# A Mamba-style decoder layer on one core: the FFN residual moved into TensorE and ScalarE, the FFN in float32, and the convolution in packed halves

## The chip, the core and the metric

The kernel runs on 1 core of one Trainium2 chip. The metric is the device time of one execution in microseconds. The kernel before takes 1060.97 us (median of 3 runs, 1060.91 to 1061.49). The engines are TensorE (PE), VectorE (DVE), ScalarE (ACT), GpSimd (POOL) and SyncE (SP), which here issues nearly all DMAs.

## The reference

Four sequences of 512 tokens and 512 features go through three blocks, each of the form `x = layernorm(x + f(x))`:

```
proj = einsum('blh,he->bel', x, W_in);  hidden, gate = split(proj)       # 1024 channels each
hidden = silu(causal_conv4(hidden) + conv_bias)                          # depthwise, 4 taps
dt, B, C = split(hidden @ W_x);  dts = softplus(dt @ W_dt + b_dt)
state[t] = exp(dts*A) * state[t-1] + dts*B*hidden;  y = sum_n state*C    # 1024 channels x 16 states
f1 = ((y + hidden*D) * silu(gate)) @ W_out                               # block 1
f2 = x @ softmax((ctx Wq + bq)(ctx Wk + bk)^T)^T                         # block 2
x_scale = max|x row|/127;  x_q = round(x/x_scale);  w_q = round(w/w_scale)   # block 3, the FFN
f3 = (x_q @ w_q^T) * x_scale * w_scale + bias
```

## The kernel before

The work of one sequence ("batch" below, 0 to 3) is cut into 32 units. A unit is 32 channels times 16 states, laid out as 128 partitions by 4 groups of 512 time steps. For each unit SP copies the step sizes and inputs of 32 channels four times over the partitions (`rep<-steps`, line 357), ACT makes `dA` with four exponentials (line 553), DVE multiplies (`dBu`, line 776, two halves) and runs the recurrence (line 784, two halves), POOL multiplies the states by C (line 447), and after four units PE adds up the states with a 0/1 matrix (`state_sum`, key `y`, lines 938 and 944). DVE finishes the four units with `hs = y * gate` (line 750).

The program is one static list of steps `(b, g)`, `g` from 0 to 31. At step g of batch b, DVE does unit 32b + g + 1 and ACT the exponentials of the unit after that. Beside them each step has "items", given by the tables `REST`, `HID_AT`, `CONV_AT` and the order in `items()`: the projections and the convolution of the batch after (`h`, `c`, `g`, `z`) and attention and FFN of the batch before (`wo`, `q`, `k`, `en`, `at`, `xt`, `av`, `qt`, `ff`). All engines walk the same list of items in order, and the four PSUM banks `dense0` to `dense3` are given to the items in turn. So an engine that is late with an item holds up everything behind it on its own queue, and a product four items later.

Parts that the change touches:

- Convolution (`c`): ACT copies the projected channels from PSUM to `pj` (line 529); PE then multiplies four 128x128 diagonal matrices of taps with `pj` shifted by 0 to 3 steps (line 975).
- FFN (`qt`, `ff`): ACT rounds the rows (`xq`, line 602), PE transposes them (`qt`), ACT turns them into bf16 integers (line 566), PE multiplies with the bf16 integer weights (`ff`), and DVE scales by row and column (line 880) and adds the residual with its row sum (line 714, `add_rows`). POOL has added the bias to the residual before (line 476). Then come the moments on ACT, `rstd` on POOL, and the normalization on ACT (line 587).
- `wp`: the first six of eight channel blocks of the last batch's output projection, added to x by DVE (line 864).
- Batch 3 has nothing beside its scan but attention and FFN of batch 2, then its own rest comes alone at the end (`REST_BESIDE`, `REST_AFTER`).

Of the kernel before, what the change touches and what calls it, by code (L numbers as in the profile page):

```python
# [5 lines left out]
ALU = mybir.AluOpType  # L6
# [5 lines left out]
P = 128  # L12
NB = 4
# [16 lines left out]
REPS = 4  # L30
RING = 6
# [11 lines left out]
REST = {"wo": [3, 3, 6, 8], "q": [2], "k": [1], "en": [5, 9, 10, 11], "at": [10, 12, 14, 14],  # L43
        "xt": [13, 13, 14, 15], "av": [15, 17, 19, 19], "qt": [18, 20, 22, 23], "ff": [19, 22, 23, 25]}
REST_BESIDE = {"q": [22], "k": [22], "en": [23, 23, 26, 27], "at": [26, 27, 28, 29], "wp": [27, 28, 29, 30]}
REST_AFTER = {"wo": [3, 4, 5, 6], "xt": [5, 6, 7, 8], "av": [6, 7, 8, 9], "qt": [9, 10, 11, 12],
              "ff": [10, 11, 12, 13]}

HID_AT = [5, 9, 11, 13, 14, 17, 19, 22]
CONV_AT = [9, 10, 13, 14, 17, 18, 21, 24]  # L50
# [18 lines left out]
def items(b, g):  # L69
# [13 lines left out]

    if after and g == (B_AT if b >= 0 else 27):
        keys.extend(("sb", b + 1, j) for j in range(NJ))
# [6 lines left out]
    if after and b >= 0:  # L92
        keys.extend(("c", b + 1, i) for i, at in enumerate(CONV_AT) if at == g)
# [4 lines left out]
    if b == LAST:  # L98
        rest(b, REST_BESIDE, ("q", "k", "at", "en", "wp"))
    if after and g == DT_AT:  # L100
        keys.append(("dt", b + 1, 0))
# [7 lines left out]
    if b == 0 and g == 4:  # L109
        keys.append(("ws", 0, 0))  # L110
    if g % 4 == SUM_AT and 0 <= n - 1 < NB * NE:
        keys.append(("y", (n - 1) // NE, (n - 1) % NE))
# [24 lines left out]
def decoder_layer(nc, x, xT, ctxT, w_in, w_conv, conv_k, conv_b, w_x, w_dt, b_dt, w_out, a_log, d_skip,  # L137
# [9 lines left out]
    with ExitStack() as ctx:  # L147
# [9 lines left out]
        WfT = sb("WfT", [P, KH, H], BF16)  # L157
        ident = sb("ident", [P, P])
        sel = sb("sel", [P, P])
# [13 lines left out]
        ws_bc = sb("ws_bc", [P, H])  # L173
# [3 lines left out]
        steps = sb("steps", [P, 3, 2, T])  # L177
# [5 lines left out]
        pj = sb("pj", [P, T])  # L183
        dA = sb("dA", [P, 2, NJ, T])
# [26 lines left out]
        xqT = small[:, 2 * T:3 * T].bitcast(BF16).rearrange("p (s k t) -> p s k t", s=2, k=KH)  # L211
        wide_scale = small[:, 0:KH * P].rearrange("p (k c) -> p k c", k=KH)
# [12 lines left out]
        xsc = sb("xsc", [P, TT])  # L225
        xinv = sb("xinv", [P, TT])
# [6 lines left out]
        s_act_c = sem("act_constants_loaded")  # L233
        s_wx = sem("wx_loaded")
# [43 lines left out]
        s_xb = sem("ffn_bias_added")  # L278
        s_ln3 = sem("ln3_done")
# [38 lines left out]
        def _(sp):  # L318
# [50 lines left out]
            for b, g in STEPS:  # L369
# [4 lines left out]
                for key in items(*STEPS[STEPS.index((b, g)) - 1]) if (b, g) != STEPS[0] else ():  # L374
                    if key[0] in "hgc":
                        load_w(wuse.index(key) + 3)
# [734 lines left out]
```

## Time and profile before

| | us |
|---|---|
| median of 3 runs | 1060.97 |
| the profiled execution | 1060.82 |
| its span in the trace | 1059.0 |
| DVE busy | 984.8 (93%) |
| PE busy | 864.7 (82%) |
| ACT busy | 806.3 (76%) |
| POOL busy | 734.5 (69%) |
| mean granted TensorE clock | 0.913 of full |

The first scan starts at 54 us and the last ends at 1009 us. The batches start their scans about 245 us apart, batch 0 after 221 us already since no batch stands before it. A row of the timeline reads: start, duration, engine, line, operation, out<-in, count, and in brackets the idle time of the engine before it with what ended that. A full-precision (float32) matmul of 512 columns shows as two records.

### The profile page before, as it was taken

What the parts mean: (1) busy time and instruction counts of PE and PEld (TensorE: products, weight loads), DVE (VectorE), ACT (ScalarE), POOL (GpSimd) and SP (SyncE); (2) the same over time, 40 slices, a digit from 0 to 9 for tenths busy, and PEclk for the clock granted to TensorE, in tenths of its full rate; (3) what the DMA queues carried; (4) which work ended last, traced back from release to release, by engine and by line L of the source; (5) the groups of instructions that cost most, each with busy time, mean ns of one, the idle gap of its engine ahead of it and who ended that gap; (6) DMA issues with size and microseconds to landing.
All of it is one profiled execution on the core that took longest, in us unless ns stands there. A gap on an engine that the chain in (4) does not pass through costs nothing.

```text
span 1059.0 us, 10554 instructions
## 1 busy us (share of the span) xinstructions
PE 864.7 (82%) x3078; PEld 352.8 (33%) x3088; DVE 984.8 (93%) x813; ACT 806.3 (76%) x1222; POOL 734.5 (69%) x260
## 2 busy tenths in 40 slices
PE   8955788876899899977699899967799576767895
PEld 3321233321344343322244344432234242323432
DVE  3699999999999999899999999899999999999747
ACT  4486788876778898998767898997876886986424
POOL 1057777777787766688778866588778867878443
PEclk9988799888899999978899999989799879878998
DMA  6255444554743344343744544344743443244001
GB/s 197 78 125 133 102 120 129 122 132 115 196 126 88 101 129 119 80 116 102 231 125 100 129 120 109 79 106 130 213 115 90 133 106 90 70 129 110 1 0 40
DMA packets 58473, 120.08 MB, mean 113 GB/s; under 512 B 12208, under 2 KB 18480, under 8 KB 58416
## 3 DMA queue, kind: packets, MB, share of 16 engines
q1 hardware_dynamic: 57696, 119.34, 43.0%
q8 instruction: 25, 0.41, 0.1%
q14 instruction: 32, 0.26, 0.1%
q10 hardware_dynamic: 720, 0.08, 0.1%
HBM read 48.07 MB, written 4.19 MB: 49 GB/s over the span
## 4 chain that ended last, share of the span: by engine, by line
DVE 32%; issue 31%; PE 18%; ACT 13%; DMA 2%; SPq 2%; POOL 2%; DVEq 0%; POOLq 0%; ACTq 0%
DVE st L784 21%; PE dense L897 10%; DVE dBu L776 7%; ACT dA L553 4%; PE dense L944 3%; ACT L553 2%; DMA rep<-steps 2%; PE dense L975 2%; SPq L357 1%; POOL st L447 1%; ACT L543 1%; DVE dense L880 1%; DVE xsc L840 1%; PE dense L926 1%; PE dense L919 1%
## 5 line engine op out<-in xcount | busy, mean ns | idle before, releaser
L447 POOL TENSOR_TENSOR st<-st,Cb 128x2048 f32<-128x2048 f32 x127 | 649.4, 5113 | 266.8 <-DVE dBu L776 265.9
L784 DVE TENSOR_TENSOR_SCAN st<-dA,dBu 128x1024 f32<-128x1024 f32 x256 | 570.1, 2266 | 0.4 <-ACT dA L553 0.4
L553 ACT ACTIVATE dA<-rep,Aneg 128x511 f32<-128x511 f32 x512 | 328.2, 710 | 53.7 <-DVE st L784 49.4
L776 DVE TENSOR_TENSOR dBu<-rep,Bb 128x1024 f32<-128x1024 f32 x256 | 305.2, 1236 | 1.9 <-DMA rep<-steps 1.9
L897 PE MATMUL dense<-xTs,Win 128*128 128x512 f32 x504 | 237.0, 617 | 7.9 <-ACT wide L558 5.1
L944 PE MATMUL dense<-st,sel 128*32 128x512 f32 x1024 | 139.2, 691 | 57.7 <-POOL st L447 57.0
L897 PEld LDWEIGHTS dense<-xTs,Win 128*128 128x128 f32 x504 | 99.8, 200 | 137.5 <-issue 136.8
L897 PE MATMUL dense<-wide,hs 128*128 128x512 f32 x256 | 114.7, 601 | 1.9 <-DVE hs L750 1.0
L553 ACT ACT_TABLE_LOAD x78 | 100.1, 1283 | 9.7 <-DVE st L784 8.5
L975 PE MATMUL dense<-pj,Win 128*128 128x512 f32 (+1 forms) x192 | 87.6, 599 | 1.7 <-ACT pj L529 0.9
L944 PEld LDWEIGHTS dense<-st,sel 128*32 128x32 f32 x1024 | 33.4, 124 | 158.3 <-issue 89.8
L465 POOL TENSOR_TENSOR rstd<-var,neghalf 128x1 f32<-128x1 f32 x48 | 36.5, 759 | 49.1 <-DVE var L733 27.5
L897 PEld LDWEIGHTS dense<-wide,hs 128*128 128x128 f32 x256 | 49.1, 194 | 63.5 <-issue 63.5
L897 PE MATMUL dense<-dt_s,Wdt 128*128 128x512 f32 x64 | 38.4, 685 | 28.0 <-ACT Bb L558 19.4
L975 PEld LDWEIGHTS dense<-pj,Win 128*128 128x128 f32 x192 | 35.2, 190 | 53.0 <-issue 53.0
L587 ACT ACTIVATE x<-x,nmean,rstd 128x512 f32<-128x512 f32 x36 | 28.6, 809 | 26.0 <-POOL nmean L467 26.0
L897 PE MATMUL dense<-wide 128*128 128x512 f32 x96 | 45.2, 621 | 0.5 <-ACT steps L543 0.5
L543 ACT ACT_TABLE_LOAD x32 | 41.1, 1283 | 0.6
L648 ACT ACT_TABLE_LOAD x32 | 41.1, 1283 | 0.6
L750 DVE TENSOR_TENSOR hs<-dense,ta 128x512 f32<-128x512 f32 x32 | 21.4, 668 | 20.9 <-PE dense L944 20.9
L938 PE MATMUL dense<-hs,Ddiag 128*128 128x512 f32 x64 | 33.3, 602 | 6.2 <-ACT Cb L558 4.4
L897 PE MATMUL dense<-hs,wide 128*128 128x512 f32 x80 | 35.8, 597 | 1.8 <-ACT hs L534 1.4
(120 smaller groups left out, 778.7 us busy)
## 6 DMA issues: line engine op xcount, KB each, us to landing
rep<-steps SPq DMA_DIRECT2D x512, 128.0 KB, 2.4
Win<-w_in SPq DMA_DIRECT2D x64, 256.0 KB, 2.9
wide<-w_out SPq DMA_DIRECT2D x4, 2048.0 KB, 9.7
Win<-w_conv SPq DMA_DIRECT2D x24, 256.0 KB, 2.9
xTs<-xT SPq DMA_DIRECT2D x3, 1024.0 KB, 5.7
x<-x SPq DMA_DIRECT2D x3, 1024.0 KB, 8.5
out<-x SPq DMA_DIRECT2D x12, 256.0 KB, 2.0
wide<-w_x SPq DMA_DIRECT2D x4, 640.0 KB, 5.0
```

The source lines that it names most:

```text
L447: nc.gpsimd.tensor_tensor(s, s, Cb[:], ALU.mult).then_inc(s_p, NH)
L465: nc.gpsimd.tensor_tensor(rstd[:, c], var[:, c], neghalf[:], ALU.pow).then_inc(s_rstd, 1)
L543: nc.scalar.activation(steps[:, n % 3, 0, :], ps, ACT.Softplus, bias=bdt[:, e:e + 1]).then_inc(free, 1)
L553: nc.scalar.activation(dA[:, u % 2, j, 1:T], rep[:, u % REPS, 0, 1:T], ACT.Exp, scale=Aneg[:, u % UNITS, j:j + 1]).then_inc(s_dA, 1)
L587: nc.scalar.activation(x_i, x_i, ACT.Identity, scale=rstd[:, n % 4:n % 4 + 1], bias=nmean[:, n % 4:n % 4 + 1]).then_inc({"wo": s_ln1, "av" ...
L648: nc.scalar.activation(temp_slot(key), ps, ACT.Silu).then_inc(free, 1)
L776: V.tensor_tensor(dBu[:, j, :], rep[:, u % REPS, 1:2, :].to_broadcast([P, JH, T]), Bb[:, j, :], ALU.mult).then_inc(s_mul, 1)
L784: V.tensor_tensor_scan(st[:, u % RING, j, :].rearrange("p j t -> p (j t)"), dA[:, u % 2, j, :].rearrange("p j t -> p (j t)"), dBu[:, j, :] ...
L897: mm = nc.tensor.matmul(ps[0:rows, :], lhsT, rhs, start=n == 0, stop=n == len(pairs) - 1)
L938: nc.tensor.matmul(ps, Ddiag[:, e, :], hs[:, b % 2, e, :], start=True, stop=False)
L944: mm = nc.tensor.matmul(ps[32 * q:32 * q + 32, :], sel[:, 0:32], st[:, (4 * n + q) % RING, j, :], start=False, stop=j == NJ - 1)
L975: mm = nc.tensor.matmul(ps[:, k:T], Win[:, n % 3, k, :], pj[:, 0:T - k], start=k == 0, stop=k == KC - 1)
```

## The change

- FFN in float32: the weights stay rounded, but are multiplied by their scale again (so they carry the column scale) and kept in float32, as are the rounded rows. The matrix `ws_bc` of column scales and its products go away.
- FFN residual, batches 0 to 2: at `qt`, ACT waits for POOL's bias add and multiplies the residual row in place by `1/x_scale` (new semaphore `s_xs`). PE adds it into the product with an identity matmul. ACT evicts the sum, scaled by `x_scale`, with its row sum. DVE has no part in it any more. Batch 3 keeps DVE's add, with the row scale in the same instruction.
- `wp`: PE adds x by an identity matmul, ACT copies the result.
- Convolution in halves: SP copies `pj` by four DMAs into `pk`, in which each half of 64 channels stands twice, the second copy shifted by one step. Two matrices of 64 output columns per half then cover four taps, so there are two pairs of 64-column matmuls instead of four of 128. Tap DMAs are half as large.
- `steps` has 2 buffers instead of 3 (`DTS`). `xqT` is twice as large and overlaps `bc_s`, so the copy `bc` waits for the last `ff` of the batch before the last.
- Tables and order: `y` now stands first in its step (it was last), `c` behind the rest, and most tables have moved by a step or so.
- The last unit's second half is multiplied by C on DVE, not on POOL.

```diff
-HID_AT = [5, 9, 11, 13, 14, 17, 19, 22]
-CONV_AT = [9, 10, 13, 14, 17, 18, 21, 24]
+HID_AT = [6, 9, 12, 13, 14, 16, 18, 21]
+CONV_AT = [9, 10, 13, 14, 16, 19, 21, 24]
...
+            def shift_taps(b, i):
+                n = NE * (b - 1) + i
+                product_read(sp, ("h", b, i))
+                if n:
+                    product_done(sp, ("c", (n - 1) // NE + 1, (n - 1) % NE))
+                else:
+                    sp.wait_ge(s_prep, 1)
+                for m in range(2):
+                    half = slice(64 * m, 64 * m + 64)
+                    sp.dma_start(pk[0:64, m, :], pj[half, :]).then_inc(s_pk, 16)
+                    sp.dma_start(pk[64:128, m, 1:T], pj[half, 0:T - 1]).then_inc(s_pk, 16)
...
                 if n:
-                    product_done(act, ("c", (n - 1) // NE + 1, (n - 1) % NE))
+                    act.wait_ge(s_pk, 64 * n)
                 nc.scalar.copy(pj[:], ps).then_inc(free, 1)
...
                     elif kind == "qt":
                         integers(key, xqT[:, i % 2])
+                        if kb < LAST:
+                            act.wait_ge(s_xb, TT * kb + i + 1)
+                            x_i = rows_of[kb][:, i, :]
+                            nc.scalar.activation(x_i, x_i, ACT.Identity, scale=xinv[:, i:i + 1]).then_inc(s_xs, 1)
+                    elif kind == "wp":
+                        copied(key, rows_of[kb][:, i, :], lambda ps: ps)
+                    elif kind == "ff" and kb < LAST:
+                        ps, free = full(key)
+                        n = norm[key]
+                        nc.scalar.activation(rows_of[kb][:, i, :], ps, ACT.Identity, scale=xsc[:, i:i + 1],
+                                             accum_out=rowsum[:, n % 4:n % 4 + 1]).then_inc(free, 1)
...
-                        link(V.scalar_tensor_tensor(ps, ps, xsc[:, i:i + 1], ws_bc[:], ALU.mult, ALU.mult))
                         dve.wait_ge(s_xb, TT * kb + i + 1)
-                        add_rows(key, x_i, ps, free)
+                        add_rows(key, x_i, ps, free, xsc[:, i:i + 1])
...
-                        for k in range(KC):
-                            mm = nc.tensor.matmul(ps[:, k:T], Win[:, n % 3, k, :], pj[:, 0:T - k],
-                                                  start=k == 0, stop=k == KC - 1)
+                        for k in range(0, KC, 2):
+                            for m in range(2):
+                                mm = nc.tensor.matmul(ps[64 * m:64 * m + 64, k:T],
+                                                      Win[:, n % 3, k // 2, 64 * m:64 * m + 64],
+                                                      pk[:, m, 0:T - k], start=k == 0, stop=k == KC - 2)
...
                         product_read(pe, ("qt", kb, i))
-                        product(key, [(xqT[:, i % 2, k, :], WfT[:, k, :]) for k in range(KH)])
+                        rows = []
+                        if kb < LAST:
+                            pe.wait_ge(s_xs, TT * kb + i + 1)
+                            rows = [(ident[:], rows_of[kb][:, i, :])]
+                        product(key, [(xqT[:, i % 2, k, :], WfT[:, k, :]) for k in range(KH)] + rows)
```

TensorE, steps 18 to 20 of batch 1 or 2, before (`small x4` is `qt`, `wide` is `av`, `WfT` is `ff`, `Ddiag` and `st,sel` are `y`, `pj` is `c`, `xTs,Win` is `h` or `g`):

```order
L919 MATMUL dense<-ident,small 128x128 x4
L897 MATMUL dense<-xTs,Win 128x512 x4
L897 MATMUL dense<-wide 128x512 x8
L897 MATMUL dense<-WfT,small 128x512 x4
L897 MATMUL dense<-xTs,Win 128x512 x4
L919 MATMUL dense<-ident,small 128x128 x4
L938 MATMUL dense<-hs,Ddiag 128x512
L944 MATMUL dense<-st,sel 32x512 x16
```

The same place in the kernel after, and on to the first `ff`, which is now at step 21:

```order
L947 MATMUL dense<-ident,small 128x128 x4
L925 MATMUL dense<-wide 128x512 x8
L1004 MATMUL dense<-pk,Win 64x512 x2
L1004 MATMUL dense<-pk,Win 64x510 x2
L925 MATMUL dense<-xTs,Win 128x512 x4
L966 MATMUL dense<-hs,Ddiag 128x512
L972 MATMUL dense<-st,sel 32x512 x16
L947 MATMUL dense<-ident,small 128x128 x4
L925 MATMUL dense<-xTs,Win 128x512 x4
L925 MATMUL dense<-WfT,small 128x512 x4
L925 MATMUL dense<-x,ident 128x512
```

Here `y` stands ahead of its step's `qt`, and `ff` has moved behind it, with the identity matmul of the residual at its end.

ScalarE, step 22 of batch 1 or 2, before (with the semaphores that each row waits for):

```order
L543 ACTIVATE steps<-dense,bdt 128x512 [waits dense_full1]
L529 COPY pj<-dense 128x512 [waits dense_full0,dense_full2]
L566 ACTIVATE small<-dense,unround 128x512 [waits dense_full3]
L553 ACT_TABLE_LOAD [waits scan_done]
L553 ACTIVATE dA<-rep,Aneg 128x511 [waits rep_loaded1]
```

The same step in the kernel after:

```order
L558 ACTIVATE steps<-dense,bdt 128x512 [waits dense_full1]
L581 ACTIVATE small<-dense,unround 128x512 [waits dense_full2]
L699 ACTIVATE x<-x,winv 128x512 [waits ffn_bias_added]
L706 ACTIVATE x,rowsum<-dense,wscale 128x512 [waits dense_full3]
L602 ACTIVATE x<-x,nmean,rstd 128x512 [waits rstd_ready]
L568 ACT_TABLE_LOAD [waits scan_done]
L568 ACTIVATE dA<-rep,Aneg 128x511 [waits rep_loaded1]
```

Two full-row instructions stand between the transposed rows and the next exponentials, and the first of them waits for POOL.

TensorE, steps 28 and 29 of batch 3, before (`ident,xTs` is `at`, `wide,hs` is `wp`):

```order
L926 MATMUL dense<-ident,xTs 128x128 x3
L929 MATMUL dense<-ident 128x128
L926 MATMUL dense<-ident,xTs 128x128
L897 MATMUL dense<-wide,hs 128x512 x6
L938 MATMUL dense<-hs,Ddiag 128x512
L944 MATMUL dense<-st,sel 32x512 x16
L926 MATMUL dense<-ident,xTs 128x128 x4
L929 MATMUL dense<-ident 128x128
L897 MATMUL dense<-wide,hs 128x512 x12
```

The same place in the kernel after:

```order
L966 MATMUL dense<-hs,Ddiag 128x512
L972 MATMUL dense<-st,sel 32x512 x16
L954 MATMUL dense<-ident,xTs 128x128 x3
L957 MATMUL dense<-ident 128x128
L954 MATMUL dense<-ident,xTs 128x128
L925 MATMUL dense<-hs,ident 128x512
L925 MATMUL dense<-wide,hs 128x512 x6
L925 MATMUL dense<-hs,ident 128x512
L925 MATMUL dense<-wide,hs 128x512 x6
```

`y` of step 28 now comes ahead of that step's transposes and output projection, which all follow it.

## Rows read from the trace of the kernel before

**Rows 1.** Stretches: start:end, length, busy PE, PEld, DVE, ACT, POOL, clock, DMA
```profile
58.40:279.50 221.10, 164.58 (x568) 60.92 (x567) 221.10 (x145) 169.14 (x221) 166.14 (x32) 0.85 0.50 129
279.50:524.80 245.30, 215.70 (x781) 88.31 (x784) 235.69 (x177) 207.98 (x321) 182.97 (x61) 0.94 0.47 123
...
770.20:994.70 224.50, 172.20 (x615) 75.07 (x618) 217.97 (x175) 170.31 (x282) 169.89 (x58) 0.88 0.38 97
291.90:483.50 191.60, 177.06 (x598) 75.78 (x599) 181.99 (x140) 167.46 (x262) 142.39 (x51) 0.96 0.43 112
```

**Rows 2.** Groups by line and form, DVE: busy us, mean ns, idle before
```profile
L880 DVE SCALAR_TENSOR_TENSOR dense<-dense,xsc,ws_bc 128x512 f32<-128x512 f32 x16 | 11.8, 738 | 7.8 <-PE dense L897 7.8
...
L714 DVE SCALAR_TENSOR_TENSOR x<-dense,x 128x512 f32<-128x512 f32 x12 | 8.3, 691 | 0.4
```

**Rows 3.** Timeline of DVE, batch 1, rows with idle time before them
```profile
374.62 0.69 DVE L750 TENSOR_TENSOR hs<-dense,ta 128x512 f32<-128x512 f32 x1 [1.98 <-PE dense L944]
...
432.21 0.76 DVE L880 SCALAR_TENSOR_TENSOR dense<-dense,xsc,ws_bc 128x512 f32<-128x512 f32 x1 [3.76 <-PE dense L897]
```

**Rows 4.** Waits of ACT from 291.9 to 483.5: us in total, times, longest
```profile
ACT small L673 <- DVE nmax L854: 3.5, 2, 2.5
...
ACT small L595 <- DVE rsum L835: 3.2, 1, 3.2
ACT small L602 <- DVE xinv L844: 2.0, 1, 2.0
```

**Rows 5.** Groups by line and form, ACT
```profile
L587 ACT ACTIVATE x<-x,nmean,rstd 128x512 f32<-128x512 f32 x36 | 28.6, 809 | 26.0 <-POOL nmean L467 26.0
...
L685 ACT ACTIVATE x<-dense 128x512 f32<-128x512 f32 x24 | 14.0, 586 | 5.9 <-PE dense L897 5.9
...
L685 ACT ACTIVATION_READ_ACCUMULATOR x<-dense 128x1 f32 x24 | 4.7, 194 | 0.0
```

**Rows 6.** Timeline of ACT and DVE: ACT's lead at both ends of the stretch
```profile
291.93 1.33 ACT L553 ACTIVATE dA<-rep,Aneg 128x511 f32<-128x511 f32 x2 [3.20 <-DVE st L784]
...
302.82 4.45 DVE L784 TENSOR_TENSOR_SCAN st<-dA,dBu 128x1024 f32<-128x1024 f32 x2
...
483.52 2.56 ACT L553 ACTIVATE dA<-rep,Aneg 128x511 f32<-128x511 f32 x4
...
492.65 4.46 DVE L784 TENSOR_TENSOR_SCAN st<-dA,dBu 128x1024 f32<-128x1024 f32 x2
```

**Rows 7.** Timeline of ACT and POOL at the second `qt` of batch 1
```profile
444.41 0.67 ACT L566 ACTIVATE small<-dense,unround 128x512 bf16<-128x512 f32 x1
...
445.63 1.27 POOL L476 TENSOR_TENSOR x<-x,small 128x512 f32<-128x512 f32 x1
```

**Rows 8.** Timeline of PE: a state sum, what follows it, a convolution
```profile
309.13 3.64 PE L944 MATMUL dense<-st,sel 128*32 128x512 f32 x32
312.70 1.13 PE L897 MATMUL dense<-small 128*128 128x512 f32 x2
...
374.48 3.69 PE L975 MATMUL dense<-pj,Win 128*128 128x512 f32 x8
```

**Rows 9.** SP's issue of one unit's four DMAs, and their landing
```profile
289.74 2.41 SPq L357 DMA_DIRECT2D rep<-steps  x4
...
rep<-steps SPq DMA_DIRECT2D x512, 128.0 KB, 2.4
```

**Rows 10.** Timeline of the end, POOL, DVE and PE
```profile
974.06 5.34 POOL L447 TENSOR_TENSOR st<-st,Cb 128x2048 f32<-128x2048 f32 x1
...
993.40 0.69 DVE L750 TENSOR_TENSOR hs<-dense,ta 128x512 f32<-128x512 f32 x1 [6.12 <-PE dense L944]
...
1013.54 1.93 PE L944 MATMUL dense<-st,sel 128*32 128x512 f32 x16 [0.40 <-POOL st L452]
...
1041.74 0.81 PE L897 MATMUL dense<-WfT,small 128*128 128x512 bf16 x3 [0.57 <-ACT small L566]
...
1052.98 0.69 DVE L714 SCALAR_TENSOR_TENSOR hs<-dense,hs 128x512 f32<-128x512 f32 x1
```

More of the change, by code:

```diff
@@ L30 @@
 REPS = 4
+DTS = 2
 RING = 6
@@ L99, in items @@
         rest(b, REST_BESIDE, ("q", "k", "at", "en", "wp"))
+    if after and b >= 0:
+        keys.extend(("c", b + 1, i) for i, at in enumerate(CONV_AT) if at == g)
     if after and g == DT_AT:
@@ L376, in _ @@
                         load_w(wuse.index(key) + 3)
+                for key in items(b, g):
+                    if key[0] == "h" and key[1]:
+                        shift_taps(*key[1:])
                 if scanned and g == 2 and b + 1 < NB:
@@ L429, in _ @@
                                     base=0, pattern=[[-1, P]], channel_multiplier=1).then_inc(s_masks, 1)
-            for n, d in enumerate(range(-3, 4)):
+            for n, d in enumerate(range(-3, 1)):
                 if n:
@@ L539, in soft @@
                 ps, free = full(("z", b, e))
-                if n >= 3:
-                    act.wait_ge(s_dA, NJ * NQ * (n - 2))
-                    act.wait_ge(s_du, n - 2)
-                nc.scalar.activation(steps[:, n % 3, 0, :], ps, ACT.Softplus, bias=bdt[:, e:e + 1]).then_inc(free, 1)
+                if n >= DTS:
+                    act.wait_ge(s_dA, NJ * NQ * (n - DTS + 1))
+                    act.wait_ge(s_du, n - DTS + 1)
+                nc.scalar.activation(steps[:, n % DTS, 0, :], ps, ACT.Softplus, bias=bdt[:, e:e + 1]).then_inc(free, 1)
             def exps(u, j):
@@ L758, in step_inputs @@
                 hidden_ready(dve, b, e)
[L759 to L760 removed]
+                if n >= DTS:
+                    for v in range(NQ * (n - DTS), NQ * (n - DTS + 1)):
                         dve.wait_ge(s_rep[v % REPS], 64 * (v // REPS + 1))
[L762 removed]
+                V.tensor_tensor(steps[:, n % DTS, 1, :], steps[:, n % DTS, 0, :], hs[:, b % 2, e, :],
                                 ALU.mult).then_inc(s_du, 1)
@@ L1013, in _ @@
                         turned(key, x1[:, i, :])
-                    elif kind == "ws":
-                        pe.wait_ge(s_wq, KH + 1)
-                        ps, done = bank_of(key)
-                        for k in range(KH):
-                            mm = nc.tensor.matmul(ps[:, k * P:(k + 1) * P], wide_scale[:, k, :], ident[:],
-                                                  start=True, stop=True)
-                        mm.then_inc(done, 1)
                     elif kind in ("wp", "wo"):
@@ L1075, in columns @@
         return v.reshape(-1, P).T
-    taps = np.zeros((NE, P, KC, P), np.float32)
+    taps = np.zeros((NE, 2, 64, 2, P), np.float32)
     for k in range(KC):
-        taps[:, range(P), k, range(P)] = a["attn_conv_kernel"][:, 0, KC - 1 - k].reshape(NE, P)
+        w = a["attn_conv_kernel"][:, 0, KC - 1 - k].reshape(NE, 2, 64)
+        for m in range(2):
+            taps[:, k % 2, range(64), k // 2, range(64 * m, 64 * m + 64)] = w[:, m]
+    taps = taps.reshape(NE, P, 2, P)
     arrays = {
```

100 lines of the change are left out of this document (47 added, 53 removed).

## The prediction

> **What bounds the kernel now.** I read the stretches by batch first. In batch 0 VectorE is busy for all of its 221.1 us; in batch 1 for 235.7 of 245.3 (batch 2 repeats batch 1), and in batch 3 for 218.0 of the 224.5 up to the last two units [rows 1]. So VectorE sets the time, and what counts is its own work plus the 9.6 us that it waits in each of batches 1 and 2. Then I read the timeline for what it waits for there: the state sum of four units, because PE takes `y` last in its step (1.98 us in the row shown, the like one sum later), and the product of the first `ff` (3.76 us) [rows 3]. TensorE is busy for 215.7 us of such a batch and ScalarE for 208.0 [rows 1], so both are near the bound in the middle of the batch, where nearly all of the side work stands.
>
> The engine that receives the new work, ScalarE, needs a closer look. At the start of the stretch from 291.9 to 483.5 it is 10.9 us ahead of the scan that needs its exponentials (291.93 against 302.82). At the end it is 9.1 us ahead (483.52 against 492.65) [rows 6]. In between it is idle for 191.6 - 167.5 = 24.1 us [rows 1], of which 3.5 + 3.2 + 2.0 = 8.7 us is waiting for VectorE's small results (row maxima, inverses) [rows 4].
>
> The sums below are made against the profiled execution, 1060.8 us (span 1059.0 and 1.8 around it), which is the median of the runs shown to 0.15 us.
>
> **The change part by part.**
>
> FFN residual off VectorE. For each of 12 row blocks 738 + 691 ns go [rows 2], 1.43 us, which is 5.7 us per batch in batches 1 to 3, all beside scans and all on the path. In batch 3 one `wp` add, of the form and size of the 691 ns add, goes as well: 0.7 us. The other three stand at the end, where VectorE waits anyway.
>
> Waits of VectorE. `ff` is taken by ScalarE, so VectorE can no longer wait for it. `y` first in its step puts it ahead of up to two products of 3.5 us, more than the 2 us waited, so those waits go too. What is late next is ScalarE. If VectorE alone set the pace, a batch would lose 5.7 + 9.6 = 15.3 us.
>
> ScalarE's side. Per batch it gains four in-place scalings of a row block (the normalization in place has that form, 809 ns) and four evictions with a row sum, 586 + 194 ns [rows 5]: 4 x 1.59 = 6.4 us. One activation-table load fewer per batch (a `c` and a gate now share a step) I take as nothing. There is a new wait: the scaling stands behind POOL's bias add. At the second `qt` ScalarE would be ready at 445.1 and POOL is done at 446.9 [rows 7], 1.8 us; the fourth is alike, the first and third find POOL done. That makes 3.6 us per batch. Behind the waiting instruction stand an `ff` eviction, a normalization and the exponentials of the unit after next.
> So between the same two exponentials ScalarE needs 167.5 + 6.4 = 173.9 us of work and 3.6 of new waits. The 8.7 us of waits for VectorE should go when ScalarE is no longer ahead; the other 24.1 - 8.7 = 15.4 us (POOL, PE, and the full lead at the start) stay. Together 192.9 us, 1.3 more than before. It can give up its lead down to two exponentials, 1.3 us [rows 6]: VectorE then needs 192.9 - 10.9 + 1.3 = 183.3 us from scan to scan, where it took 492.65 - 302.82 = 189.8. **Gain 6.5 us in each of batches 1 and 2.** Ends: if the 8.7 us stay as well, a loss of 2.2 us; if ScalarE's waits for PE shrink so far that VectorE binds, a gain of 15.3. I take 6.5 since it is what the rows give when only waits for the faster engine vanish.
>
> Batch 3 has fewer side items (no `h`, no `c`): ScalarE is busy 170.3 of 224.5 us [rows 1], so its 6.4 us more are covered. Gain 5.7 + 0.7 = 6.4 us. Between nothing (if the new wait binds) and 6.4 I take all of it. Batch 0 has no FFN beside it and VectorE never waits [rows 1]: nothing.
>
> TensorE. `ff` in float32 with an identity product is five full products. Four take about 3.5 us (the convolution's eight records, 3.69 with the tail of the last, which the next product overlaps [rows 8]), so 4.4 us instead of about 0.9, and 14 us more per batch. The convolution halves, if two 64-column matmuls run side by side as four 32-column ones do: 32 records in 3.6 us instead of 14 [rows 8]. That saves 1.6 us each, 13 us per batch. Both about cancel, but the convolutions lie in front of the crowded steps 18 to 20 and the `ff` now behind them. Bounds for the convolution: nothing saved (a rival below), or 1.75 each. I take 1.6.
> A change from full width to column pieces costs something: from the start of the state sum to the start of the next product it is 312.70 - 309.13 = 3.57 us, under 0.2 more than the 3.4 to 3.5 us of eight full records [rows 8]. Two such changes per convolution cost at most 0.3 of the 1.75 us that halving saves. The Trainium skill, TensorEngine Tiling (Array Packing), section Key Properties, speaks against this part: changing the tiling mode drains the engine. By the trace the drain is small, and by the rule with that price or by ignoring it the sum is the same, since PE does not bind.
>
> The relay through SP. Each convolution now waits for four DMAs, 2.4 us to issue and 2.4 to land [rows 9]. SP first waits for ScalarE's copy and for the convolution before, and the `rep` copies of the next unit queue behind. By the order, seven of eight convolutions have two or more product groups between the one before and themselves, over 4 us. Cost 0, between 0 and 4.8 us each. If that cover is gone, a rival follows. Two `steps` buffers in place of three: the exponentials waited for were issued on ScalarE's own queue before, so nothing. Head: eight short roundings instead of eight shorter ones, before the first `rep` has landed: nothing.
>
> The end. In step 28 VectorE waits 6.12 us for `y` [rows 10], which PE has behind a transposed block and `wp`. Now `y` can start when POOL is done, at 974.06 + 5.34 = 979.4. But all `wp` work follows it: 3.6 (y) + 1.1 + 2 x 6.1 (two `wp` of seven products) + 1.1 + 6.1 + 3.5 + 0.9 + 3.6 gives 1011.5 for the last state sum (1.1 for a block of five quarter-width matmuls), against 1013.54 + 1.93 = 1015.5: 4.0 us gained. POOL and VectorE would be ready some 3 us before that, also since they share the last unit. Then `ff` in float32 is bare: starting at 1041.74, four products of 3.5 us and two `qt` of 0.5 end at 1056.7, where VectorE took the last add at 1052.98 [rows 10]: 3.7 us lost. Net gain 0.3; ends -4 and +4.
>
> Sum: 2 x 6.5 + 6.4 + 0.3 = 19.7 us. 1060.8 - 19.7 = **1041 us**.
>
> **The rivals.**
> - VectorE binds throughout. For: ScalarE's waits for PE come from products that now stand elsewhere, and PE is relieved in steps 9 to 18. Against: the new 1.6 us per row block fall on steps 18 to 25, where ScalarE's lead is already under the 10.9 us it starts with. Time: 2 x 15.3 + 6.4 + 0.3 = 37.3 us less, 1023.
> - ScalarE keeps all its waits. For: row maxima and inverses are needed within the step in which they are made, whoever is ahead. Time: 2 x 2.2 more, 6.7 less: 1058.5.
> - The halves do not run side by side (the change doesn't do what it says). The state sum shows four pieces of 32, no row shows two of 64. PE then has 13 us per batch more, 229 busy in about 239; if half of it becomes waits, 2 x 6.5 more than forecast: 1054.
> - Slower, by the relay. If nothing covers the 4.8 us, eight per batch are 38.4 us on PE's queue: 217 + 38 = 255 us instead of 245.3, `y` late for VectorE with it. Twice +10, less 6.7: 1074. It decides once more than 28 us of a batch's relays (3.5 us each) are uncovered. For: PE's queue is in order, so a late convolution holds `y`. Against: the order, as said.
>
> **How the numbers follow.** Forecast 0.42, VectorE bound 0.25, ScalarE keeps its waits 0.13, no packing 0.10, relay 0.10. About 0.2% (2 us) is what a measurement can tell from no change: the first, second and fourth are faster, the third lies at that edge and is split, the last is slower. Faster 0.83, same 0.06, slower 0.11. The range takes in the second and most of the third: 1023 to 1057. The forecast's own range is 1034 to 1048.
>
> **What would show it.** Right: no row of VectorE waiting for the state sum or `ff` in batches 1 and 2, but waits of its scans for `dA` late in these batches, together 5 to 10 us each; VectorE's busy time about 23 us lower in all (17.1 for the residual, 2.8 for `wp`, 3.0 for the four scalings at the end); a convolution's eight records in about 1.9 us; the scaling waiting for POOL about twice per batch; the last state sum ending PE-bound and the last `ff` about 4 us longer after the `qt`. Wrong: batch 1 as long as before or over 8 us shorter; a convolution waiting for its halves by more than 1 us in more than a few places; batch 0 longer than 221 us; scans waiting for `rep`.

## The result and the profile after

The kernel after takes 1064.1 us (median of 12 runs) against 1061.6 for the kernel before in the same comparison: ratio 1.0021, interval 1.0011 to 1.0030. So it is slightly slower, by about 2 us, where 1041 was predicted. Its profiled execution has a span of 1062.7 us, 3.7 more than before.

The same stretches as in [rows 1], of the kernel after: batches 0 to 3 up to the start of unit 126, then the end (columns as there):

```profile
58.70:280.90 222.20, 154.78 (x560) 52.72 (x559) 221.16 (x144) 166.42 (x219) 166.01 (x32) 0.82 0.58 143
280.90:524.10 243.20, 215.61 (x808) 85.48 (x808) 235.78 (x165) 211.46 (x332) 179.05 (x61) 0.96 0.55 137
...
768.90:989.50 220.60, 178.92 (x636) 77.64 (x637) 214.95 (x161) 175.23 (x295) 169.96 (x58) 0.88 0.39 98
989.50:1062.70 73.20, 65.02 (x204) 29.19 (x202) 40.30 (x95) 24.35 (x36) 26.71 (x31) 0.98 0.04 15
```

Batch 1 lasts 243.2 us instead of 245.3. VectorE's busy time in it, the third busy column, is 235.8 against 235.7 [rows 1], although 5.7 us of FFN work left it. Its waits went from 9.6 to 7.4 us. Batch 3 is 3.9 us shorter up to unit 126, and the end, 64.3 us before (994.7 to 1059.0), is 8.9 longer.

What took the place of the 5.7 us is seen when the dBu multiply is read alone. Its busy time by batch, before (L776) and after (L803), after start:end and length:

```profile
279.50:524.80 245.30, 76.92 (x64) 0.94 0.47 123
```
```profile
280.90:524.10 243.20, 82.47 (x64) 0.96 0.55 137
```

The same 64 multiplies take 5.55 us more. The timeline shows which (start, us, engine, line; the timeline of VectorE shows the two halves of a unit as one row, x2):

```profile
455.93 0.29 ACT L595 ACTIVATE var<-rowsq,eps 128x1 f32<-128x1 f32 x1
456.31 0.55 POOL L480 TENSOR_TENSOR rstd<-var,neghalf 128x1 f32<-128x1 f32 x1 [3.26 <-ACT var L595]
...
457.07 1.26 POOL L491 TENSOR_TENSOR x<-x,small 128x512 f32<-128x512 f32 x1
...
458.30 4.52 POOL L463 TENSOR_TENSOR st<-st,Cb 128x2048 f32<-128x2048 f32 x1
458.70 0.72 ACT L699 ACTIVATE x<-x,winv 128x512 f32<-128x512 f32 x1
...
459.51 5.29 PE L925 MATMUL dense<-WfT,small 128*128 128x512 f32 x8 [5.32 <-ACT x L699]
459.59 5.46 DVE L803 TENSOR_TENSOR dBu<-rep,Bb 128x1024 f32<-128x1024 f32 x2
...
469.88 3.64 PE L972 MATMUL dense<-st,sel 128*32 128x512 f32 x32
...
473.59 0.69 DVE L777 TENSOR_TENSOR hs<-dense,ta 128x512 f32<-128x512 f32 x1 [3.58 <-PE dense L972]
```

Read it downwards. ScalarE finishes the moments of a row block at 456.2. POOL needs them for the inverse deviation, which stands on its queue ahead of the bias add and of the multiply of states by C, and has waited 3.3 us. So the multiply starts at 458.30 and still runs when VectorE begins the next unit's pair of dBu multiplies: that pair takes 5.46 us, not 2.36. Now the rows of PE. It stands still for 5.3 us before the batch's third `ff` (459.51), which starts behind ScalarE's scaling (458.70). POOL's bias add is done by then (458.33). It is ScalarE's own queue that is late: the transposed rows, which this `ff` needs as well, are made only from 458.13 to 458.81. While PE idles its clock is granted in full; once it starts again it is not:

```profile
454.00:459.40 5.40, 0.20 (x2) 0.00 (x0) 5.40 (x4) 5.31 (x11) 3.02 (x4) 1.00 0.99 255
459.50:462.50 3.00, 2.98 (x4) 1.45 (x5) 3.00 (x2) 2.97 (x5) 3.00 (x1) 0.50 0.67 197
```

At 0.50, the lower of the clock's two levels, for these 3 us, the eight records of this `ff` take 5.29 us; those of the `ff` before (449.23) take 3.67. The state sum is queued behind, and VectorE waits 3.6 us for `y` at 473.59.

POOL's waits for these moments, over the whole run (us in total, times, longest), after and then before:

```profile
POOL rstd L480 <- ACT var L595: 61.4, 24, 5.4
```
```profile
POOL rstd L465 <- ACT var L580: 21.5, 11, 3.5
```

Other steps in the profile after: VectorE waits for `ff` no more in batches 1 and 2, but for `y` 24.6 us in eight places (20.9 before). Where PE comes to a convolution without a pause its eight records take 1.94 us, as forecast in answer to [rows 8]. At the end the state sum is bound by PE, and the add of the last `ff` lies 41.2 us behind the last `y`, 37.4 before [rows 10]:

```profile
473.45 1.94 PE L1004 MATMUL dense<-pk,Win 128*64 128x512 f32 x8
...
1011.66 3.64 PE L972 MATMUL dense<-st,sel 128*32 128x512 f32 x32
...
1015.37 0.69 DVE L777 TENSOR_TENSOR hs<-dense,ta 128x512 f32<-128x512 f32 x1 [8.93 <-PE dense L972]
...
1056.58 0.75 DVE L741 SCALAR_TENSOR_TENSOR hs<-dense,wscale,hs 128x512 f32<-128x512 f32 x1 [1.50 <-PE dense L925]
```

The relay shows too. The last of four copies is issued at 354.02, and the convolution starts at 357.09, when PE has been idle for 4.2 us ("issue" means that the profile names no releaser; but the copy landed at 357.00):

```profile
354.02 0.60 SPq L371 DMA_DIRECT2D pk<-pj  x1
...
357.09 3.54 PE L1004 MATMUL dense<-pk,Win 128*64 128x512 f32 x8 [4.22 <-issue]
```

Six of the 24 convolutions, the second and third of each batch, start 0.1 us after the landing of their last copy, with PE idle for 1.5 to 4.2 us before, 16.1 us in all. This one ran at a granted clock of 0.53 and took 3.54 us, so there the halves saved nearly nothing. Five of the 24 took 3.3 to 3.7 us, all of them after PE had been idle for 2.0 us or more, and 19 took 1.94.

### The profile page after: what moved, and what is told of

It is laid out like the page before. It is cut to its first block, busy times and chain, and to the rows that moved or that the text cites. A ratio compares the mean times of both kernels' runs of the same rounds, so it can differ in the third digit from the quotient of the medians.

```text
span 1062.7 us, 10837 instructions
## 1 busy us (share of the span) xinstructions
PE 880.9 (83%) x3176; PEld 351.2 (33%) x3176; DVE 981.1 (92%) x771; ACT 817.7 (77%) x1258; POOL 722.6 (68%) x256
## 4 chain that ended last, share of the span: by engine, by line
issue 29%; DVE 25%; PE 23%; ACT 15%; SPq 3%; DMA 3%; POOL 1%; DVEq 0%; ACTq 0%; POOLq 0%
DVE st L811 17%; PE dense L925 16%; DVE dBu L803 5%; ACT dA L568 5%; PE dense L972 3%; ACT L568 2%; DMA rep<-steps 2%; SPq L357 2%; PE dense L1004 2%; ACT L558 1%; ACT squares L592 1%; ACT L549 1%; ACT steps L558 1%; DVE steps L789 1%; PE dense L966 1%
## 5 line engine op out<-in xcount | busy, mean ns | idle before, releaser
L463 POOL TENSOR_TENSOR st<-st,Cb 128x2048 f32<-128x2048 f32 x127 | 641.7, 5052 | 230.8 <-DVE dBu L803 230.7
L803 DVE TENSOR_TENSOR dBu<-rep,Bb 128x1024 f32<-128x1024 f32 x256 | 320.0, 1293 | 0.6 <-DMA rep<-steps 0.6
L972 PE MATMUL dense<-st,sel 128*32 128x512 f32 x1024 | 126.9, 640 | 45.8 <-POOL st L463 45.8
L480 POOL TENSOR_TENSOR rstd<-var,neghalf 128x1 f32<-128x1 f32 x48 | 38.9, 810 | 101.0 <-ACT var L595 61.4
L1004 PE MATMUL dense<-pk,Win 128*64 128x512 f32 (+1 forms) x192 | 54.5, 694 | 23.6 <-issue 16.1
L925 PE MATMUL dense<-WfT,small 128*128 128x512 f32 x128 | 64.4, 651 | 11.1 <-ACT x L699 10.6
L777 DVE TENSOR_TENSOR hs<-dense,ta 128x512 f32<-128x512 f32 x32 | 21.4, 668 | 25.4 <-PE dense L972 24.6
L925 PEld LDWEIGHTS dense<-WfT,small 128*128 128x128 f32 x128 | 25.8, 210 | 42.7 <-issue 30.9
L602 ACT ACTIVATE x<-x,nmean,rstd 128x512 f32<-128x512 f32 x36 | 28.8, 808 | 13.8 <-POOL nmean L482 13.8
```

The source lines that it names most:

```text
L463: nc.gpsimd.tensor_tensor(s, s, Cb[:], ALU.mult).then_inc(s_p, NH)
L480: nc.gpsimd.tensor_tensor(rstd[:, c], var[:, c], neghalf[:], ALU.pow).then_inc(s_rstd, 1)
L602: nc.scalar.activation(x_i, x_i, ACT.Identity, scale=rstd[:, n % 4:n % 4 + 1], bias=nmean[:, n % 4:n % 4 + 1]).then_inc({"wo": s_ln1, "av" ...
L803: V.tensor_tensor(dBu[:, j, :], rep[:, u % REPS, 1:2, :].to_broadcast([P, JH, T]), Bb[:, j, :], ALU.mult).then_inc(s_mul, 1)
L925: mm = nc.tensor.matmul(ps[0:rows, :], lhsT, rhs, start=n == 0, stop=n == len(pairs) - 1)
L972: mm = nc.tensor.matmul(ps[32 * q:32 * q + 32, :], sel[:, 0:32], st[:, (4 * n + q) % RING, j, :], start=False, stop=j == NJ - 1)
```

## The experiments

The theory: ScalarE, with its added work, delivers the moments later; POOL, which needs them ahead of its multiply, runs into VectorE's next dBu multiplies and stretches them, and PE, waiting for ScalarE's scaling, delivers `y` late. The rivals: the relay of the convolution through SP costs; the new order costs; ScalarE sets the pace whatever POOL does.

| run | us | before, same chip | ratio | interval |
|---|---|---|---|---|
| after | 1064.1 | 1061.6 | 1.0021 | 1.0011 to 1.0030 |
| e1_pool_early | 1532.5 | 1060.5 | 1.4452 | 1.4430 to 1.4473 |
| e2_rstd_free | 1050.7 | 1060.5 | 0.9903 | 0.9888 to 0.9918 |
| e3_no_scaling | 1052.9 | 1060.5 | 0.9924 | 0.9909 to 0.9939 |
| e4_ffn_dve | 1050.1 | 1060.5 | 0.9888 | 0.9870 to 0.9906 |
| e5_conv_plain | 1072.5 | 1062.2 | 1.0101 | 1.0084 to 1.0117 |
| e6_y_last | 1085.2 | 1062.2 | 1.0221 | 1.0205 to 1.0236 |
| e7_packed_only | 1082.5 | 1062.2 | 1.0194 | 1.0179 to 1.0210 |
| e8_old_ffn | 1048.2 | 1062.2 | 0.9866 | 0.9852 to 0.9881 |
| e9_after_late | 1057.7 | 1062.0 | 0.9960 | 0.9946 to 0.9975 |
| e10_old_ffn_late | 1048.1 | 1062.0 | 0.9869 | 0.9853 to 0.9884 |
| e11_ffn_dve_late | 1050.1 | 1062.0 | 0.9888 | 0.9873 to 0.9904 |
| e12_order_only | 1055.7 | 1062.0 | 0.9942 | 0.9926 to 0.9958 |

Differences from the kernel after below are differences of ratios times 1061 us.

**The collision by itself**, in the kernel before:

```diff
                     pool.wait_ge(s_scan, NH * (u + 1))
-                    if step_inputs_at(u + 1):
-                        pool.wait_ge(s_mul, NH * (u + 2))
-                    else:
-                        pool.wait_ge(s_mul, NH * (u + 2) - 1)
```

> The kernel before with one wait less: POOL multiplies a unit's states by C as soon as the scan is done, not only after VectorE has multiplied dBu of the next unit. Its 4.5 us multiply then always runs beside VectorE's dBu multiplies. Theory 'collision' (VectorE's dBu multiply is stretched while POOL's two-input multiply runs; in the kernel after single ones took 4.32 us instead of 1.24): the mean of a dBu multiply rises from 1.24 us to over 2 us, VectorE's busy time by over 150 us, and the kernel is slower by 100 to 400 us, although y comes earlier. Rival 'no collision' (the long multiplies of the kernel after have another cause): the mean stays below 1.3 us and the time within 5 us of 1061.

It is 472 us slower. The group of dBu multiplies (busy, mean ns), and a place in the timeline:

```profile
L772 DVE TENSOR_TENSOR dBu<-rep,Bb 128x1024 f32<-128x1024 f32 x256 | 798.8, 3163 | 2.0 <-DMA rep<-steps 2.0
```
```profile
615.47 4.50 POOL L443 TENSOR_TENSOR st<-st,Cb 128x2048 f32<-128x2048 f32 x1 [6.74 <-DVE st L780]
...
616.23 5.97 DVE L772 TENSOR_TENSOR dBu<-rep,Bb 128x1024 f32<-128x1024 f32 x2
```

VectorE's pair, begun at 616.23, ends at 622.20, that is 2.23 us after POOL's multiply (619.97), about the 2.36 that a pair takes undisturbed: while POOL multiplies, VectorE makes next to no progress. The scans, between these rows, keep their 2.26 us each. So the one wait that this run leaves out is what keeps the two apart, and it says only when POOL may begin, not when it must.

**POOL no longer held by the moments**, in the kernel after:

```diff
-                        pool.wait_ge(s_var, n + 1)
-                    nc.gpsimd.tensor_tensor(rstd[:, c], var[:, c], neghalf[:], ALU.pow)
+                        if n >= 4:
+                            normalized(pool, norm_keys[n - 4])
+                        nc.gpsimd.tensor_tensor(rstd[:, c], ones[:, 0:1], neghalf[:], ALU.pow)
...
-                    nc.gpsimd.tensor_tensor(nmean[:, c], nmean[:, c], rstd[:, c], ALU.mult)
+                        nc.gpsimd.tensor_tensor(rstd[:, c], ones[:, 0:1], rstd[:, c], ALU.mult)
```

> The kernel after, in which POOL's inverse deviation of batches 0 to 2 is made from a constant instead of the variance (the normalization's scale is then not the reference's), so that POOL never waits for ScalarE's moments before its multiply; all instructions and sizes stay. Theory 'POOL held by the moments': the stretched dBu multiplies of batches 1 and 2 go (L803 from 320 us to about 306 in all) and part of VectorE's waits for y with them, 1064 - 14 to -22 = 1042 to 1050. Rival 'ScalarE sets the pace' (the late POOL is a symptom only, the waits move to dA): over 1058. Rival 'relay of the convolution': no change, 1064.

12.5 us less than after, just short of what was expected. Batch 1 and the dBu multiplies in it:

```profile
280.90:521.00 240.10, 216.16 (x808) 86.51 (x808) 230.27 (x165) 211.28 (x332) 186.35 (x61) 0.96 0.56 139
```
```profile
280.90:521.00 240.10, 77.07 (x64) 0.96 0.56 139
```

VectorE's work in the batch is now 5.4 us below that of before, as the prediction had it. ScalarE's is unchanged to 0.2 us, so its load alone did not set the pace. The part on `y` was wrong: VectorE's waits for it in the whole run are 26.7 us, no less than 24.6. So a late POOL is not what makes `y` late.

**ScalarE's scaling left out:**

```diff
-                            act.wait_ge(s_xb, TT * kb + i + 1)
-                            nc.scalar.activation(x_i, x_i, ACT.Identity, scale=xinv[:, i:i + 1]).then_inc(s_xs, 1)
...
-                            pe.wait_ge(s_xs, TT * kb + i + 1)
+                            pe.wait_ge(s_xb, TT * kb + i + 1)
```

> The kernel after without ScalarE's scaling of the residual rows by the inverse row scale (left out, so the FFN's residual has the wrong size; PE waits for POOL's bias add instead). It takes away 12 x 0.8 = 9.5 us of ScalarE's work and 26.5 us of its waits for POOL. Theory 'ScalarE is late with moments, so POOL is late': part of the stretched dBu multiplies and of the waits for y and ff go, 1051 to 1058. Rival 'relay' or 'order of y': within 2 us of 1064. Rival 'ScalarE sets the pace all along': 1064 - 9.5 - up to 26 = 1040 or less.

10.3 us less, in the expected range. POOL waits 48.7 us for moments instead of 61.4, and the dBu mean is 1264 ns instead of 1293. (ScalarE's scaling had waited 15.3 us for POOL, not 26.5 as the expectation has it.) PE still stands idle for 4.7 us before the third `ff` of a batch, now for the transposed rows, instead of 5.3: of that pause the scaling made only 0.6 us, and VectorE's waits for `y` fall only to 22.5 us.

**FFN residual back on VectorE:**

```diff
-                    elif kind == "ff" and kb == LAST:
+                    elif kind == "ff":
...
-                            pe.wait_ge(s_xs, TT * kb + i + 1)
-                            rows = [(ident[:], rows_of[kb][:, i, :])]
```

> The kernel after with the FFN residual of batches 0 to 2 back on VectorE (one add of 0.69 us with the row scale in the same instruction, as batch 3 has it), no scaling and no eviction on ScalarE, and no identity product on PE; FFN in float32, the order, the packed convolution and wp stay. VectorE gains 12 x 0.69 = 8.3 us of work, ScalarE loses 12 x 1.59 = 19 us and its 26.5 us of waits for POOL, PE 12 x 0.9 = 11 us. Theory 'ScalarE late, POOL late, collision': VectorE gets back about 10 to 14 us of stretched multiplies and some waits for y and ff, 1055 to 1062. Rival 'VectorE's own work binds, as the prediction had it': 1064 + 8.3 = 1072. Rival 'relay or order': 1064 to 1072.

14.1 us less than after, more than expected, with the row add and its scale (736 ns) back on VectorE. The mean of a dBu multiply falls to 1243 ns, POOL's waits for moments to 36.1 us, and the waits for `y` to 16.4:

```profile
DVE hs L767 <- PE dense L962: 16.4, 5, 7.9
```

The third `ff` stands behind the same pause (5.1 us) at a low clock, and some of the wait changes its name: VectorE now waits 5.8 us for `ff` in batches 1 and 2. So moving 12 adds off the busiest engine costs 14 us here.

**Packing undone in the kernel after** (`c` ahead of `h` again):

```diff
-                    if key[0] == "h" and key[1]:
-                        shift_taps(*key[1:])
...
-                        pe.wait_ge(s_pk, 64 * (NE * (kb - 1) + i + 1))
+                        product_read(pe, ("h", kb, i))
...
+                        for k in range(KC):
+                            mm = nc.tensor.matmul(ps[:, k:T], Win[:, n % 3, k, :], pj[:, 0:T - k],
```

> The kernel after with the convolution undone: four 128x128 tap matrices on pj, no relay through SP and no pk; the convolution stands ahead of h in its step again. PE gains about 1.7 us per convolution, 13.6 us per batch. Theory (packing helps, PE is near the bound in batches 1 and 2 and late products make ScalarE, the moments and POOL late): slower than after by 4 to 15 us, 1068 to 1079. Rival 'the relay costs' (waits for the four DMAs and fuller SP and DMA queues took the gain): 1062 or faster.

8.5 us slower than after. PE is busy 225.5 us in batch 1 instead of 215.6. Packing and relay together are no cause of the loss.

**`y` last in its step, in the kernel after** (the same two lines further down in `items()`):

```diff
-    if g % 4 == SUM_AT and 0 <= n - 1 < NB * NE:
-        keys.append(("y", (n - 1) // NE, (n - 1) % NE))
     if after and g == (B_AT if b >= 0 else 27):
```

> The kernel after with y as the last item of its step again, as in the kernel before; everything else stays. Theory (y first saves VectorE waits for y; in the kernel after they are 24.6 us, the end's 8.9 among them): they grow by 5 to 12 us and the time by about as much, 1069 to 1076. Rival 'y first holds up the products that ScalarE needs' (late POOL, then late y, then late everything on PE's queue): at most 1064, faster by up to 6.

21 us slower than after, beyond the range. VectorE's waits for `y` grow from 24.6 to 53.0 us:

```profile
DVE hs L777 <- PE dense L972: 53.0, 9, 10.3
```

Batch 0 is 9 us longer too. The new tables need `y` in front.

**Packing alone in the kernel before** (as in the diff of the change: `shift_taps`, `pk`, `DTS`, the halves in PE's `c`; tables and `items()` untouched):

```diff
+                    if key[0] == "h" and key[1]:
+                        shift_taps(*key[1:])
```

> The kernel before with the packed convolution alone (relay through SP, pk, two steps buffers), in the order of before: FFN, residual, wp and the place of y as before. It takes 13.6 us per batch off PE. Theory: VectorE's waits for y and ff in batches 1 and 2 (8 us each) shrink, 1060.5 less 3 to 9: 1051 to 1057. Rival 'relay': a convolution waits for its halves and y behind it, 1061 to 1070.

20 us slower; both expectations missed, the direction of the relay rival was right. In the old order a convolution follows its `h` closely. The copy `pj` is written at 423.6, SP issues the four copies up to 426.6, then the four `rep` and only then the next weights:

```profile
423.58 0.58 ACT L549 COPY pj<-dense 128x512 f32<-128x512 f32 x1
...
424.18 0.50 SPq L374 DMA_DIRECT2D pk<-pj  x1
...
426.00 0.60 SPq L375 DMA_DIRECT2D pk<-pj  x1
...
426.72 2.48 SPq L361 DMA_DIRECT2D rep<-steps  x4
...
428.73 3.51 PE L997 MATMUL dense<-pk,Win 128*64 128x512 f32 x8 [6.47 <-DMA pk<-pj]
...
444.03 0.76 DVE L901 SCALAR_TENSOR_TENSOR dense<-dense,xsc,ws_bc 128x512 f32<-128x512 f32 x1 [7.76 <-PE dense L918]
```

PE idles 6.5 us, and the first `ff` behind it keeps VectorE waiting 7.8 us (3.8 before [rows 3]). Ten of the 24 convolutions start like this, 0.1 us after their last copy has landed, with 39.6 us of idle PE in all (16.1 in six in the kernel after). Eight of them then take 3.5 to 3.7 us instead of 1.94 (the one shown at a granted clock of 0.54), so they lose what the halves should save as well.

**Old FFN, residual and `wp`; new order and packing** (the edit of the run before, and the tables and `items()` of the kernel after):

```diff
+REST = {"wo": [3, 3, 6, 7], "q": [2], "k": [3], "en": [4, 7, 10, 11], "at": [9, 11, 13, 14],
+        "xt": [13, 14, 14, 17], "av": [15, 17, 19, 19], "qt": [18, 20, 22, 23], "ff": [21, 22, 23, 25]}
```

> The kernel before with the packed convolution and with the tables and order of the kernel after (y first), but with its own FFN: bf16 integers, column scales and residual on VectorE, wp added by VectorE, POOL's last half as before. Against the run with the float32 FFN and a residual on VectorE (1050.1): VectorE has 12 x 0.74 = 8.9 us more work, the end is 3.8 us shorter. Theory (VectorE's own work counts one to one where POOL is in time): 1050 + 8.9 - 3.8 = 1055, within 3. Rival 'PE's relief decides' (3.5 us less for each ff): 1050 or less.

1048.2 us: by the ratios 14.2 us faster than before and 16.4 faster than after. The theory (1052 to 1058) missed and the rival, that PE's relief decides, was right: VectorE's 8.9 us more work are more than paid back. A short bf16 `ff` behind the pause on PE takes 1.9 us at the low clock, the float32 one of the kernel after 5.3 to 6.1. It is the fastest of all, together with the run that adds the later deviations to it. In batch 1 VectorE is idle for 4.0 us, where it was for 9.6; 3.6 of them are waits for `y`, which were 4.3 before, and the waits for `ff` (3.8) and for ScalarE (1.1) are gone:

```profile
279.80:521.10 241.30, 206.78 (x784) 81.04 (x784) 237.28 (x177) 206.70 (x320) 183.72 (x61) 0.93 0.54 138
```

**Deviations behind POOL's multiply, nothing left out:**

```diff
+def is_late(key):
+    return key[0] in ("wo", "ff") and key[1] < LAST
...
                 for key in rows:
-                    ...
+                    if not is_late(key):
+                        deviations(key)
...
                     weigh_states(u)
+                for key in behind:
+                    deviations(key)
...
-                        ends.setdefault(s + NORM_LAG, []).append(key)
+                        ends.setdefault(s + NORM_LAG + is_late(key), []).append(key)
```

> The kernel after with nothing left out: for the norms of wo and ff in batches 0 to 2 (24 of 36) POOL makes the inverse deviation behind its multiply of that step instead of ahead of it, and ScalarE normalizes one step later; the other 12 (av) stay. Theory 'POOL held by the moments, collision': most stretched dBu multiplies go (mean from 1.293 to under 1.26 us) and the time falls by 6 to 12 us against after, 1052 to 1058. Rival 'it was ScalarE that set the pace, and the run with a constant gained by freeing the normalization too': 1062 or more, since ScalarE's queue gets no shorter.

6.5 us less than after and faster than before; the rival is out. POOL's waits for moments fall from 61.4 to 19.6 us, the dBu mean to 1264 ns. That is about half of what the run with a constant gained: the 12 deviations of `av` still come first, and POOL's bias add, which reads two tensors as well, runs into the dBu multiplies (begun beside a pair at 453.4 us, it took 2.27 us instead of 1.26 and the pair 3.41). The third `ff` still has 5.3 us of idle PE before it. Nor does the gain lie where the theory looked for it: in batch 1 the multiplies took 2.9 us less, but the waits for `y` grew by 3.4 (that `ff` took 6.56 us here), and the batch is 0.5 us longer. Batch 2 gains 1.7 us, batch 3 and the end 4.6.

**The same delay on the two fast versions:**

> The run with the old FFN, packed convolution and new order (1048.2), with the same delay of the inverse deviations. There the dBu multiplies took 309.3 us, 4.8 more than the 304.5 without collisions. Theory: 1 to 5 us less, 1043 to 1047. Rival: the later normalization costs as much elsewhere, 1048 or more.

> The run with the float32 FFN and a residual on VectorE (1050.1), with the same delay. Its dBu multiplies took 307.1 us, 2.6 over 304.5. Theory: 0 to 3 us less, 1047 to 1050. Rival: 1050 or more.

No difference can be measured in either (ratios 0.9869 against 0.9866, and 0.9888 against 0.9888), so both rivals hold by the time. POOL's waits for moments did fall, from 24.4 to 17.0 us and from 36.1 to 16.5, but the dBu multiplies hardly moved (309.3 to 307.4 us, 307.1 to 309.8). So POOL's waiting alone is no measure of the loss; what counts is whether it pushes the big multiply into VectorE's.

**The order alone** (the last but its packing; `c` ahead of `h`):

```diff
+HID_AT = [6, 9, 12, 13, 14, 16, 18, 21]
+CONV_AT = [9, 10, 13, 14, 16, 19, 21, 24]
```

> The kernel before with the tables and the place of y of the kernel after, and nothing else: its own convolution (ahead of h in its step), FFN, residual and wp. Against the run with the packed convolution as well (1048.2). In the kernel after undoing the packing cost 8.5 us. Theory 'both parts count': PE has 13.6 us more per batch, 1048 + 8.5 = 1057, a little faster than before. Rival 'the order is all': 1048 to 1051. Rival 'the order pays only with the packing': 1060 or more.

0.9942: the order alone gives 6 us, the packing on top of it 8 more (0.9866). "Both parts count".

## Why the prediction was wrong

By stretch, in us against the kernel before (profiled executions):

| | forecast | kernel after | POOL freed (run with a constant) |
|---|---|---|---|
| batch 0 and ahead of it | 0 | +1.4 | +1.4 |
| batch 1 | -6.5 | -2.1 | -5.2 |
| batch 2 | -6.5 | -0.6 | -5.8 |
| batch 3 and the end | -6.7 | +5.0 | -1.1 |
| sum | -19.7 | +3.7 | -10.7 |

So with POOL freed 14.4 of the 23.4 us that are missing come back. That run frees ScalarE's normalizations as well (they wait 4.5 us for POOL instead of 13.8), and the delay that leaves nothing out gets back only half as much, so 14.4 is what the late moments cost at most. Of the other 9.0 us more than half (5.6) lie in batch 3 and the end.

- **The step that failed: ScalarE's side, "Gain 6.5 us in each of batches 1 and 2".** It asked only whether ScalarE's exponentials come in time, and they do: VectorE's scans waited 1.2 us for `dA` in the whole run. But ScalarE's lead was used by another consumer. The moments go from ScalarE to POOL, ahead of the multiply whose end and whose collisions VectorE feels. The gains were 2.1 and 0.6 us. With POOL freed they are 5.2 and 5.8 (240.1 and 239.6 us against 245.3 and 245.4), near 6.5, though by another sum than mine: the forecast kept ScalarE as the limit at the end of the stretch, but what was gained is VectorE's own work (5.4 of the 5.7 us), with its waits unchanged. That the size came near 6.5 is luck.
- **"Those waits go too".** They did not: 9.6 us became 7.4 in batch 1. `y` first does not remove even its own waits: the two of 2.0 and 2.2 us before are 2.4 and 1.2 now, and 2.3 and 1.3 with the old FFN. What goes in the new order is the wait for `ff`. With the float32 `ff` a third wait for `y` comes in its place (3.6 us at 473.59, 4.4 in batch 2), because PE, after its pause, needs 5.3 to 6.1 us for the eight records and 1.0 for the identity product. I had taken 4.4 us for an `ff` wherever it stands. The scaling has little part in that pause (0.6 us of 5.3); its waits for POOL on ScalarE, forecast as 3.6 us per batch, are 15.3 over three batches.
- **Batch 3, "Gain 5.7 + 0.7 = 6.4".** From unit 97 to 123 it is 1.6 us longer than before. VectorE's busy time there did fall, by 3.6 us (the dBu multiplies are 0.8 us more, and one more row maximum, 0.7, falls into the stretch). But it never waited there before and now idles 5.6 us: PE, with the float32 `ff` ahead of `q`, `k` and `en`, lets it wait 4.3 us for the row maxima (`en` is the `xTs` product at 947.45). Freeing POOL does not help (4.5 us). With the residual on VectorE, and the same float32 `ff` in that place, the wait is 0.3 us, so the identity products or ScalarE's added work have a part in it; no run takes these apart. Here, too, I had counted VectorE's work alone.

```profile
943.15 3.60 PE L925 MATMUL dense<-WfT,small 128*128 128x512 f32 x8
...
947.45 1.02 PE L925 MATMUL dense<-xTs 128*128 128x512 f32 x2
...
948.50 0.69 DVE L890 TENSOR_REDUCE nmax<-dense 128x1 f32<-128x512 f32 x1 [4.31 <-PE dense L925]
```

- **Packing, 1.6 us per convolution.** Right where PE runs on: 1.94 instead of 3.69 us in 19 of 24. The other five took 3.3 to 3.7 us, which the forecast did not have. The price of changing the array's layout is small, as said.
- **The relay.** Right in sum for the new order, where undoing packing and relay costs 8.5 us, but "Cost 0" was not: six convolutions waited 1.5 to 4.2 us, where the order was to leave one per batch uncovered. The rival's price is real, and its condition was set too high: it was to decide once more than 28 us of a batch's relays are uncovered, and in the old order with packing about 10 us of idle PE in batch 1 and as much in batch 2 were enough to lengthen each by 9 us.
- **The end, net 0.3.** Sizes right, seen without the collisions: from unit 123 to the last `y` the run with a constant takes 46.1 us against 50.1 (-4.0 predicted), and from there on 47.3 against 43.5 (+3.7 predicted). In the kernel after it is 49.5: one multiply of unit 123, at 965.84, took 3.65 us instead of 1.24, and 1.0 us more went in waits. The old `wp` and FFN do better at the first and as well as before at the second: 43.5 and 43.5.
- **Its own signs of being wrong.** Two showed: batch 0 took 222.2 us, not 221, and six convolutions waited for their halves by more than 1 us. Two signs of being right did not: scans waited for `dA` 1.2 us in all and not 5 to 10 in each batch, and VectorE's busy time fell by 3.7 us and not by 23 (by 19.5 with POOL freed).
- **The rivals.** None held. VectorE does bind, but with added time of its own. The one slower than before was the relay, and the kernel is slower for another reason.

Of the whole, FFN, residual and `wp` cost 16.4 us, order and packing gave 14.2: +2.2. By itself the float32 FFN looks like the smaller part: with the residual on VectorE it costs 2.3 us against the old FFN (0.9888 against 0.9866), hardly more than the intervals allow to tell. But that is a net figure: the run with the old FFN also does 8.9 us more on VectorE and has the old `wp`, and still wins. What stays open: how much of the 14 us between the kernel after and the residual on VectorE is `y` and how much collision. The dBu multiplies are 12.9 us shorter (320.0 against 307.1), the waits for `y` 8.2 and for the row maxima 4.0; the adds take 8.8 back and the waits for `ff` 5.8. No run takes these apart.

## What to carry over

Before moving work to an engine that has a lead, list everyone who consumes its results, not only the consumer on the path: here a 128x1 result for a third engine decided. An order kept by "not before" waits protects two engines from each other only as long as neither is late. A relay through a DMA queue is priced by what stands between producer and consumer: the same packing gives 8 us in one order and costs 20 in another. And price a product on an engine that has just been idle by rows that follow such a pause: here the same eight records took 3.6 us without one and 5.3 to 6.1 behind it.

## What the runs showed of the hardware

POOL's 128x2048 multiply (4.5 us, both inputs in SBUF) and VectorE's 128x1024 multiply of two SBUF tensors (1.23 us alone) do not share: in the overlaps shown here the one that comes second waits for the first. In the timeline of the collision by itself VectorE's pair ended 2.23 us after POOL. The other way round POOL's multiply, begun while a dBu multiply runs, is listed with 5.34 instead of 4.51 us. Scans, whose second input is in PSUM, took 2.26 to 2.27 us in every kernel. The Trainium skill, SBUF — State Buffer, section SBUF: two separate sides, agrees with this: an operation of VectorE with two SBUF inputs and one of GpSimd that reads SBUF lock a shared pair of ports, and the later one is blocked for the whole instruction. I had not weighed this rule in the prediction; applied to a late POOL it gives, by POOL's 4.5 us, up to 4.5 us per collision as an estimate; the longest dBu multiply measured was 4.33 us in the kernel after and 5.55 in the run with the collision by itself, 3.1 and 4.3 over the undisturbed 1.22.

Two 64-column matmuls run side by side in float32: eight records in 1.94 us, where eight of 128 columns take 3.69.

TensorE's granted clock fell to 0.50 of full (the lower of its two levels) when it took up work again after idle stretches: behind 5.3 us at 459.5, and with a mean of 0.53 behind 4.2 us at 357.1. It came back within the same product in the first case (0.95 from 462.5 to 465.0).
